# Token rows and router logits from one product, and register loads of four items without checks, in a two-layer metaformer with experts

## What is computed

```python
x = norm(x1)                                  # each token over its 128 channels, no weights
logits = x @ router_w.T                       # 8 experts in layer 0, 16 in layer 1
top_vals, top_idx = top_k(logits, 2)
weights = softmax(top_vals)
# layer 0: gelu(x @ w1[e] + b1[e]) @ w2[e] + b2[e]         hidden width 512
# layer 1: (silu(x @ gate[e]) * (x @ up[e])) @ down[e]     hidden width 256
x = x1 + sum over a token's two experts of weight * expert(x)
```

## Time and profile before

| | |
|---|---|
| runs of the kernel before | 468.22, 469.77, 463.9 us; median 468.22 |
| the profiled execution | 468.1 us, its span 466.0 us |
| mean granted TensorE clock | 0.906 of full speed |
| busy: PE, PEld, DVE, ACT, POOL | 86%, 72%, 51%, 41%, 41% of the span |
| token stages | from 146.0 to the first gather at 169.8, and from 323.4 to 350.3 |
| expert loops | to the last scatter, at 259.8 and 448.2 |

### The profile page before, as it was taken

The page is one execution under the profiler, slowest core; times in us unless marked ns, Lnnn a source line. Parts: engine busy times, 40 slices in busy tenths (PEclk is TensorE's granted clock), DMA queues, the critical chain, the costliest instruction groups (busy, mean ns, idle before and its releaser), DMA issues.

```text
span 466.0 us, 8714 instructions
## 1 busy us (share of the span) xinstructions
PE 398.7 (86%) x2635; PEld 336.5 (72%) x2635; DVE 237.1 (51%) x584; ACT 189.9 (41%) x441; POOL 191.6 (41%) x206
## 2 busy tenths in 40 slices
PE   7996999999788969999999399898894889888823
PEld 4565999999576838999999254675663888887822
DVE  3604444561254525656666283574672555565615
ACT  4495223223121275777566173563152233222104
POOL 9952344460003037777754200001107775555530
PEclk9997999999979967999999797999865899999985
DMA  4032253442376036981100420000021211110126
GB/s 148 1 69 44 46 86 64 81 81 33 43 230 179 1 109 188 276 239 52 47 36 34 138 66 1 1 0 2 0 89 42 56 50 39 42 42 35 42 87 211
DMA packets 44019, 35.32 MB, mean 76 GB/s; under 512 B 3800, under 2 KB 39752, under 8 KB 43976
## 3 DMA queue, kind: packets, MB, share of 16 engines
q1 hardware_dynamic: 36208, 24.60, 19.9%
q0 software_dynamic: 4096, 8.40, 5.8%
q10 hardware_dynamic: 3672, 1.77, 2.5%
HBM read 21.12 MB, written 7.34 MB: 61 GB/s over the span
## 4 chain that ended last, share of the span: by engine, by line
PE 65%; DVE 10%; ACT 8%; issue 6%; DMA 5%; DVEq 3%; ACTq 1%; POOL 1%; SPq 0%; POOLq 0%
PE bank L1316 15%; PE bank L1207 11%; PE bank L1333 8%; PE bank L1166 3%; DVE w_block L951 2%; PE bank L1060 2%; DMA ln_sq<-y 2%; PE bank L1359 2%; ACT heads L543 2%; DVEq L947 2%; PE bank L1241 2%; PE bank L1253 2%; PE bank L1077 2%; PE bank L1245 1%; PE bank L1260 1%
## 5 line engine op out<-in xcount | busy, mean ns | idle before, releaser
L1316 PE MATMUL bank<-x_cols,w_block 128*128 (+1 forms) x688 | 103.0, 295 | 15.7 <-DVE w_block L951 10.9
L1316 PEld LDWEIGHTS bank<-x_cols,w_block 128*128 128x128 f32 x688 | 88.2, 201 | 26.2 <-issue 24.3
L482 POOL DMA_INDIRECT x_rows<-tok,token x64 | 62.1, 970 | 60.8 <-DMA tok<-ln_sq 41.6
L489 POOL DMA_INDIRECT y<-wide,dest x64 | 62.5, 977 | 46.1 <-DVE wide L983 40.3
L1333 PE MATMUL bank<-w_down,h_cols 128*128 (+1 forms) x500 | 70.3, 277 | 0.8 <-DVE wide L983 0.8
L1333 PEld LDWEIGHTS bank<-w_down,h_cols 128*128 128x128 f32 x500 | 62.9, 193 | 1.2 <-DVE h_cols L966 0.7
L1207 PE MATMUL bank<-cmap,cw 128*128 128x112 f32 (+2 forms) x480 | 58.9, 280 | 0.3 <-DVE router_c L793 0.3
L1207 PEld LDWEIGHTS bank<-cmap,cw 128*128 128x128 f32 x480 | 57.4, 198 | 0.4 <-DVE router_c L793 0.4
L312 POOL TENSOR_TENSOR cw<-pw_in,dw_band 128x640 f32<-128x640 f32 x24 | 37.2, 1571 | 44.1 <-PE bank L1207 38.4
L476 POOL MEMSET wide<- 128x4096 f32 x2 | 7.0, 3512 | 105.4 <-DVE xs L1034 63.7
L958 DVE TENSOR_TENSOR h_in<-bank,wT 128x512 f32<-128x512 f32 x39 | 27.0, 692 | 30.4 <-PE bank L1316 19.7
(11 more groups left out here) (209 smaller groups left out, 630.2 us busy)
## 6 DMA issues: line engine op xcount, KB each, us to landing
cmap<-heads SPq DMA_DIRECT2D x48, 64.0 KB
w_up<-in_L_ffn_w_dram SPq DMA_DIRECT2D x1, 2048.0 KB, 8.6
tok<-ln_sq SPq DMA_DIRECT2D x8, 256.0 KB, 2.2
w_up<-in_L_ffn_gate_w_dram SPq DMA_DIRECT2D x4, 512.0 KB
w_up<-in_L_ffn_up_w_dram SPq DMA_DIRECT2D x4, 512.0 KB
w_down<-in_L_ffn_down_w_dram SPq DMA_DIRECT2D x4, 512.0 KB
wide<-y SPq DMA_DIRECT2D x8, 256.0 KB, 4.2
ln_sq<-y SPq DMA_DIRECT2D x8, 256.0 KB, 4.6
```

Source lines behind the costliest of these rows:

```text
L482: pool.indirect_dma_start(out=x_rows[:, j % RING, :], out_offset=None, in_=tok_dram[r], in_offset=bass.IndirectOffsetOnAxis(ap=token[r][:, ...
L489: pool.indirect_dma_start(out=y_dram[r], in_=y_acc[:, s * C:(s + 1) * C], in_offset=None, out_offset=bass.IndirectOffsetOnAxis(ap=dest[r][ ...
L1316: mm = pe.matmul(bank[2 + j % 2][:, i * 128:(i + 1) * 128], w_block[:, j % 3, i * 128:(i + 1) * 128], x_cols[:, bass.ds((j - e[j]) * 128, ...
```

## The change

**Token stage.** `cent`, `rows`, `var`, router_c and their semaphores go. Each tile of 128 tokens gets one product with the matrix tok_w, which holds the centring matrix and beside it the centred router weights: 128 + 8 columns in layer 0, 128 + 16 in layer 1. Three tiles share a bank (six banks; `ROW_BANKS`, `row_tile`). ScalarE copies the logits of each bank out into tok_lg, squares each tile with the accumulated sum in tok_ss, and takes the roots from there; VectorE's router waits for all six logit copies. The table of places goes to bank 0, and `keep_clock` stands at both ends of `slots`.

**Register loads.** A second table holds each item's block offset (block times 128), made by VectorE behind the experts (two operations, one of which was in `item_masks`). `item_load` reads four items' values of one table by one TENSOR_LOAD, and no check or assertion follows. TensorE loads block offsets ahead of the up product and experts ahead of the down product; VectorE loads experts at the head of an iteration and block offsets ahead of the sum; ScalarE loads experts.

```diff
+        def item_load(engine, which, r, what, n, NI, most):
+
+            k = min(LOADS, NI - n)
+            return engine_values(which, items[r][0:1, what, n:n + k], most)
+
+        def engine_values(which, table, most):
+
+            return nc.values_load_multi_w_load_instructions(
+                table, engines=(which,), min_val=0, max_val=most,
+                skip_runtime_bounds_check_because=IN_BOUNDS)[1]
+
+        ROW_BANKS = ((4, 5, 6, 7, 2, 3), (4, 5, 6, 2, 7, 3))
+
+        def row_tile(r, i):
+
+            n = C + (E0, E1)[r]
+            return bank[ROW_BANKS[r][i // 3]][:, (i % 3) * n:(i % 3 + 1) * n]
+
+        ROW_GROUPS = [range(3 * g, min(3 * g + 3, TT)) for g in range(6)]
...
+                def squares(tiles):
+                    for i in tiles:
+                        act.activation(ln_sq[:, i * 128:(i + 1) * 128], row_tile(r, i)[:, 0:C], ACT.Square,
+                                       accum_out=tok_ss[:, i:i + 1]).then_inc(tok_sqd, 1)
+
+                def roots(h):
+                    act.wait_ge(tok_sqd, TT * r + 8 * h + 8)
+                    act.activation(tok_std[:, 8 * h:8 * h + 8], tok_ss[:, 8 * h:8 * h + 8], ACT.Sqrt,
+                                   scale=1.0 / C, bias=eps[:, 1:2]).then_inc(tok_root, 1)
+
+                for g, tiles in enumerate(ROW_GROUPS):
+                    act.wait_ge(rows_mm, 6 * r + g + 1)
+                    a, n = tiles[0], len(tiles)
+                    src = bank[ROW_BANKS[r][g]][:, 0:n * (C + E)].rearrange("p (t q) -> p t q", t=n)
+                    act.activation(tok_lg[:, a:a + n, 0:E], src[:, :, C:C + E], ACT.Copy).then_inc(tok_logits, 1)
+                    if g < 4:
+                        squares(tiles)
+                    if g == 3:
+                        roots(0)
+                squares(range(12, TT))
+                roots(1)
...
+                    if i % 8 == 0:
                         act.wait_ge(tok_scale, 2 * r + i // 8 + 1)
-                    act.activation(ln_sq[:, i * 128:(i + 1) * 128],
-                                   bank[4 + i // 4][:, (i % 4) * 128:(i % 4 + 1) * 128], ACT.Copy,
+                    act.activation(ln_sq[:, i * 128:(i + 1) * 128], row_tile(r, i)[:, 0:C], ACT.Copy,
                                    scale=tok_inv[:, i:i + 1]).then_inc(rows_copied, 1)
...
-                dve.tensor_copy(expert[r][:, :], item[0:1, 0, 0:NI]).then_inc(rt_table, 1)
+                dve.tensor_copy(items[r][:, EXPERT, 0:NI], item[0:1, 0, 0:NI]).then_inc(rt_table, 1)
+                step(dve.tensor_tensor(b_f, item_id[:, 0:NI], e_f, ALU.subtract))
+                dve.tensor_scalar(items[r][:, BLOCK, 0:NI], item[0:1, 1, 0:NI], float(NB - 1), 128.0, ALU.min, ALU.mult)\
+                    .then_inc(rt_table, 1)
...
-                        e[j] = dve.value_load(expert[r][0:1, j:j + 1], min_val=max(0, j - NB + 1), max_val=min(E - 1, j))
+                        if j % LOADS == 0:
+                            for i, v in enumerate(item_load(dve, mybir.EngineType.DVE, r, EXPERT, j, NI, E - 1)):
+                                e[j + i] = v
...
+                        if j % LOADS == 0:
+                            for i, v in enumerate(item_load(dve, mybir.EngineType.DVE, r, BLOCK, j, NI, (NB - 1) * C)):
+                                at[j + i] = v
                         ej = e.pop(j)
                         mask = item[:, 4, j:j + 1]
-                        acc = y_acc[:, bass.ds((j - ej) * C, C)]
+                        acc = y_acc[:, bass.ds(at.pop(j), C)]
                         dve.wait_ge(m.down, j + 1)
...
-                row = (0, E0)[r]
-
-                def cent(c):
-                    if c >= 1:
-                        pe.wait_ge(tok_sqd, NCH * r + c)
-                    pe.matmul(bank[3][:, :], center[:, :], chunk(xs, c), start=True, stop=True).then_inc(tok_cent, 1)
-
-                def rows(c):
-                    for i in range(4):
-                        mm = pe.matmul(bank[4 + c][:, i * 128:(i + 1) * 128],
-                                       xs[:, (4 * c + i) * 128:(4 * c + i + 1) * 128], center[:, :],
+                pe.wait_ge(router_out, 3)
+                for g, tiles in enumerate(ROW_GROUPS):
+                    for i in tiles:
...
+                        if i % 4 == 0:
+                            pe.wait_ge(*ready(i // 4))
+                        mm = pe.matmul(row_tile(r, i), xs[:, i * 128:(i + 1) * 128], tok_w[:, r, 0:C + E],
                                        start=True, stop=True)
                     mm.then_inc(rows_mm, 1)
-
-                def var(c):
-                    pe.wait_ge(tok_sqd, NCH * r + (c + 1, NCH)[c // 2])
-                    for i in range(4 * c, 4 * c + 4):
-                        mm = pe.matmul(bank[3 * (c // 2)][:, 256 + i:257 + i], ln_sq[:, i * 128:(i + 1) * 128], mean_w[:, :],
-                                       start=True, stop=True)
-                    mm.then_inc(tok_var, 1)
-
-                for c in range(NCH):
-                    pe.wait_ge(*ready(c))
-                    for i in range(4 * c, 4 * c + 4):
-                        mm = pe.matmul(bank[0][:, i * E:(i + 1) * E], xs[:, i * 128:(i + 1) * 128],
-                                       router_c[:, row:row + E], start=True, stop=True)
-                    mm.then_inc(rt_mm, 1)
-                for c in (0, 1):
-                    cent(c)
-                    rows(c)
-                slots(r, E, (lambda: (var(0), var(1), cent(2), rows(2), cent(3), rows(3), var(2), var(3))))
-
-            def slots(r, E, between):
+                keep_clock(0, 2)
+                slots(r, E)
+
+            def slots(r, E):
...
-                        e[j] = pe.value_load(expert[r][0:1, j:j + 1], min_val=max(0, j - NB + 1), max_val=min(E - 1, j))
+                        if j % LOADS == 0:
+                            for i, v in enumerate(item_load(pe, mybir.EngineType.PE, r, BLOCK, j, NI, (NB - 1) * 128)):
+                                at[j + i] = v
...
-                                           x_cols[:, bass.ds((j - e[j]) * 128, 128)],
+                                           x_cols[:, bass.ds(at[j], 128)],
...
+                        if j % LOADS == 0:
+                            for i, v in enumerate(item_load(pe, mybir.EngineType.PE, r, EXPERT, j, NI, E - 1)):
+                                e[j + i] = v
```

59 lines of the change are left out of this document (29 added, 30 removed).

## The result

The changed kernel takes 452.59 us (median of 451.42, 454.22, 447.65 and 453.75) where the kernel before takes 468.96 in the same comparison: ratio 0.9647, 95% interval 0.9583 to 0.9711. The profiled execution is that of 451.42 us, its span 449.6. The forecast was 451.5.

What follows compares the result with a forecast made beforehand. It took ScalarE's row scaling to bound the token stages, and circles with VectorE's register work the expert loops. Terms -6.0 - 5.8 - 4.8 = -16.6 from 468.1 gave 451.5 us; range 445 to 473, the forecast's own 447 to 458.

Steps and rivals of the forecast that it cites:

- Token stages: Both layers, first token product to first gather: -6.0 us together, bounds -2.8 and -8.
- the square with accumulation: ScalarE in the token stages: 0.32 us a tile, estimated from the exponential's 0.46 less 0.133 for 128 columns.
- L: Time of one register load of four values in the expert loops: 0.31 us taken, bounds 0.31 and 1.23.
- B: Rival on the expert loops' loads: one memory trip for each value, L = 0.78, 464.8 us in all; chance 0.36.
- C: Rival on the expert loops' loads: four values cost four loads, L = 1.23, 483.5 us in all; chance 0.11.
- Layer 0's loop: Expert loop of layer 0: items at 1.96 us in the first stretch, 1.83 later; -5.8 us.
- the circle through VectorE: Layer 0's loop: dependency round over two items, up product, bias add, gelu, next up product; 4.01 us to 3.6 to 3.65.
- Layer 1's loop: Expert loop of layer 1: items at 1.83 us in the first stretch, 1.65 later; -4.8 us.
- Nothing late next: Expert loops: GpSimd's gathers stay ahead (last block some 5 us early, loop wins 2.3); scatters stay under an item's time.
- First gathers: Sign of being right: the first gathers of layers 0 and 1 come 2.8 and 11.8 us earlier.
- Rival D: Expert loops: neither load is seen, items at 1.80 us in layer 0, 1.53 late in layer 1; 446 us; chance 0.07.
- E: Expert loops: TensorE's own sequencer sets the pace, they give 5 of 10.6 us; 457 us; 0.46 together with the forecast.

Runs made afterwards that it cites:

- one_value_loads: The changed kernel with LOADS = 1, one value per register load wherever needed, still without checks: 455.94 us, ratio 0.9727 to the kernel before.
- unchecked_alone: The kernel before with one edit: each item's expert is still loaded singly, but no check or assertion follows: 459.62 us against 473.58, ratio 0.9702.
- the next edit: The changed kernel with the second reciprocal of the roots moved right behind the first: 449.48 us, ratio 0.9480 to the kernel before.
- weights_later: The changed kernel with SyncE's transfers of layer 1's weights held back until all 32 blocks of layer 0 are turned: 447.47 us against 469.87, ratio 0.9572.
- four_trips_vector: The changed kernel with four one-value loads in place of each load of four, on VectorE only: 489.71 us, ratio 1.0475 to the kernel before.

## Why the prediction held, point by point

The total was right (451.5 forecast, 452.59 measured), the parts less so, and that the total agrees to 1.1 us is luck: the terms for the touched stages were too small by 3.7 us, and after's untouched stages ran 3.9 us longer than those of before's. With untouched stages as long as before's the profiled execution would have taken some 447.5.

- *Token stages, forecast -6.0, measured -8.1.* The term that was mis-sized is the square with accumulation: 0.32 forecast, 0.25 measured. Its deduction of 0.133 us for 128 columns stands in no row; ScalarE's copies of 256 and of 128 columns differ by 0.11 (0.385 and 0.271 in the profile of before), and with that the term would have been 0.35, further off. So a square is cheaper than the exponential's row for another reason, which no run shows. Hence the router is 4.81 behind the first product, not 5.9, and the last row tile 4.3 and 4.1 us earlier, not 2.8 and 3.2. The mechanism is as described: no reciprocal waits, half of the rows are scaled early, and the tail is 8 tiles (2.18).
- *L, forecast 0.31, measured 0.342.* It decided between the rivals, and B (0.78) and C (1.23) fall with it. What the forecast did not separate is the checks from the loads, which it charged as one gap: one_value_loads and unchecked_alone show that 8.5 and 10.1 of the loops' 12.2 us come without loading four at a time. The Trainium skill (Runtime: NRT & Kernel Launch, section on instruction fetch mechanics) puts a register load at about 200 ns per register "even for bulk". From the page's figure comes an estimate of 0.8 us for four and 1.6 for eight; measured are 0.342 and 0.602. For a table in SBUF, as here, the measurement decides.
- *Layer 0's loop, forecast -5.8, measured -5.2.* First stretch 1.97 (1.96 forecast). Late 1.79 where 1.83 was forecast: not the circle through VectorE sets it but TensorE, whose two products leave no gap, at the 1.78 that the prediction gave for TensorE alone. The bias add starts 0.15 behind the up product's end (235.78, 235.93), 0.28 in an item with a load; 0.2 was forecast.
- *Layer 1's loop, forecast -4.8, measured -7.0.* Late 1.60 (1.65), early 1.76 (1.83). The loads were right: 0.24 + 0.26 in the passage, 0.29 + 0.20 forecast. The circle without loads was not: 3.06 forecast, 2.86 from 405.04 to 407.90: half of the difference is the weight block, which follows 0.26 behind the sum and not 0.36, the other half h_cols, which starts 1.61 behind the up product where it started 1.71 before.
- *Nothing late next.* True for GpSimd. But the profile of before had the transfers of the weights in it, and the forecast did not ask what an earlier loop would do to them. In the changed kernel there is one wait of 0.55 us for a block, in the next edit one of 4.77, and with the transfers held back (weights_later) none but the wait for the first block.
- *First gathers, forecast 2.8 and 11.8 us earlier.* In absolute times the first came 2.45 us later and the second 9.6 earlier. By this sign alone the forecast would have looked wrong; the distance from the first token product was the right thing to name.
- *Rival C's working*, made true by four_trips_vector, gave 483.5 with the squares' loss in it. It took 489.7 without that loss. Layer 0's term was right, layer 1's too small by some 16 us (122.6 measured, 106 worked out), of which the clock can explain 13 at most by the estimate above.
- *Rival D*, loads unseen, did not happen in layer 1 (the passage shows 0.24 and 0.26); layer 0's pace is near its 1.80, but TensorE sets it. *E*, TensorE holds the pace, happened in layer 0 alone and at a pace no worse than the circle's.
- *The touched stages' share.* The prediction says about two thirds of the span. Their 238.6 us are 51% of 466.0. No term of the sum rests on it.

## What to carry to other kernels

Look at what stands around a register load before counting loads: here the bounds check and assertion behind it cost more than the load, a load of one or four values hides for a quarter to a third of its time (0.21 of 0.306 and 0.25 of 0.342 show) behind the operation that runs, and loads spread over items cost little where the same loads in one place cost 42 us. Work out a stage's gain as a distance between marks within it, since the same code ahead of it took 146 to 153 us with different courses of the granted clock; and look at the clock within the stage as well. And when a loop starts earlier, list the transfers that its own progress sets off.

## What was not expected of the hardware

- A TENSOR_LOAD from the table in SBUF takes 0.306 us for one value, 0.342 for four and 0.602 for eight on VectorE: three more values add 0.036, the next four 0.26.
- Ten idle times of 2.0 to 2.6 us on TensorE in one loop came with a granted clock of 0.79 in six stretches of 8 us.
- Three transfers of 512 KB, issued within 1.5 us, came with a gathered block that took 8.0 us from its issue to its use, in place of 2.9; TensorE waited 4.77 us for it. With the transfers held back the wait was gone.
- TensorE's clock in the first 30 us took different courses in executions of the same code, and the first token stage then began at 146.0 to 152.4 us with the code of before and at 147.5 to 152.8 with that of after.
